# Storing the last sample of a four-layer convolution kernel in sixteen blocks instead of one transfer

## The chip, the cores and the metric

The kernel runs on one core of a Trainium2 chip. The metric is the device time of one execution in microseconds (us), lower being better. The engines are named as in the profile: PE (TensorE, matrix multiplication), DVE (VectorE), ACT (ScalarE), POOL (GpSimd) and SP (SyncE, which here only issues transfers). Each has its own instruction stream, and they meet at semaphores. SP and ACT can both issue DMAs, each on a queue of its own; the profile calls these instructions SPq and ACTq DMA_DIRECT2D.

## The reference

The input is x, eight samples of 16 channels of 128x128 float32. Four residual layers follow one another, each on a group-normalised copy of x:

```python
x = x + _L0_conv_ref(_gn(x), ...)   # 3x3 conv, kernel mixed per sample from 3 experts
x = x + _L1_conv_ref(_gn(x), ...)   # abs, then 3x3 depthwise conv
x = x + _L2_conv_ref(_gn(x), 8)     # 17x17 box mean
x = x + _L3_conv_ref(_gn(x), ...)   # neighbour sums, then five 1x1 convs, elu between them
```

In the last layer the sums of the eight neighbours go through four 64-wide layers with elu, and a fifth that is averaged and scaled down to 16 channels. Only its result, added to x, completes an output sample. The output has the shape of x, 1 MB per sample.

## The kernel before, in words

All eight samples stay in one SBUF tile `xs` of 128 partitions. A partition holds one channel c and one residue r of the image row modulo 8 (`R = 8`, `C = 16`), and in it lie `K = 16` rows of 128 values for each sample. The layout of a sample in DRAM, seen the same way, is `ov` (L209): r, c, k, w, in which one run of adjacent bytes is one image row of 512 bytes. A sample is worked on in `Q = 4` quarters of `KB = 4` such rows per partition.

The work is a software pipeline over samples, written out by hand for every engine in a function `one(t)` that `rounds` calls (L288): round t finishes sample t-1's last layer while the earlier layers of samples t, t+1 and t+2 run beside it. In the last round (t = 8) only the last layer of sample 7 is left. That layer goes, for each quarter and each of its layers, from PE (`layer`, L764) to ACT and DVE (`elu`, L646, and `join`, L979), and back to PE. The fifth layer is `last_layer` (L785), and `output` (L989) on DVE adds its result into `xs` and increments `out_evac`. Quarters 0, 1 and 2 of the last sample are written by DVE inside the last round; the fourth comes after it, as the last instruction of the DVE stream.

SP issues the transfers in this order: within a round the load of a later sample, the store of an earlier one, then the windows and stacks that spread neighbouring rows over partitions. `store(j)` (L387) waits until all four quarters of sample j are in `xs` and then issues one DMA of the whole sample:

```python
def store(j):
    sp.wait_ge(out_evac, Q * j + Q)
    sp.dma_start(ov[j] if isinstance(j, int) else ..., xs[:, bass.ds(j * N, N)]...).then_inc(out_stored, 16)
```

Sample 6 is stored in the last round, and `store(B - 1)` for sample 7 stands behind `rounds` (L430). The last wait of SP (L431) is for all eight stores. ACT's stream ends with its part of the last round; it issued DMAs only during the start of the kernel.

Of the kernel before, what the change touches and what calls it, by code (L numbers as in the profile page):

```python
# [16 lines left out]
B, C, H, W = 8, 16, 128, 128  # L17
R = 8
K = H // R
P = R * C  # L20
N = K * W
Q = 4
KB = K // Q
# [52 lines left out]
def build(nc, x, w_experts, conv_bias, fc_w, fc_b, w_depth, w1, w2, w3, w4, w5, con_early, con_channel, con_late, out):  # L76
    with ExitStack() as ctx:
        def sb(name, shape, dtype=F32):
            return ctx.enter_context(nc.sbuf_tensor(name, shape, dtype))
# [4 lines left out]
        def sem(name):  # L84
            return ctx.enter_context(nc.semaphore(name))
# [6 lines left out]
        xs = sb("xs", [P, B * N])  # L92
# [112 lines left out]
        out_evac = sem("out_evac")  # L205
        out_stored = sem("out_stored")

        xv = x.rearrange("b c (k r) w -> b r c k w", r=R)
        ov = out.rearrange("b c (k r) w -> b r c k w", r=R)  # L209
# [26 lines left out]
        LOAD = 16  # L236
# [37 lines left out]
        def loaded(i):  # L274

            return LOAD if isinstance(i, int) and i == 0 else LOAD * (i + 2)

        def has(i):

            return not isinstance(i, int) or 0 <= i < B  # L280
# [7 lines left out]
        def rounds(eng, one):  # L288

            one(1)  # L290
            with eng.Fori(2, B - 3) as t:
                one(t)
            for t in range(B - 3, B + 1):
                one(t)
# [32 lines left out]
        def windows0(eng, i, halves, last):  # L327

            for h in halves:
                eng.wait_ge(y0_written, Y0 * i + Y0 // 2 * (h + 1))  # L330
                for dst, rows in around(y0, win0, h, False):
                    eng.dma_start(dst, rows).then_inc(win0_in, 16)
                dst, rows = ((win0[1][3 * C:4 * C, K - 1:K], y0[6 * C:7 * C, K - 1:K]) if h else
                             (win0[0][0:C, 0:1], y0[C:2 * C, 0:1]))
                eng.dma_start(dst, rows).then_inc(win0_in, 16)
            if last:
                eng.wait_ge(y0_written, Y0 * i + Y0)
                for h in range(2):
                    for dst, rows in around(y0, win0, h, True):
                        eng.dma_start(dst, rows).then_inc(win0_in, 16)  # L340

        def windows1(eng, i, halves, last):

            for h in halves:
                eng.wait_ge(y1_written, Y1 * i + 2 * h + 2)
                for dst, rows in around(y1, win1, h, False):
                    eng.dma_start(dst, rows).then_inc(win1_in, 16)
            if last:
                eng.wait_ge(y1_written, Y1 * i + Y1)
                for h in range(2):  # L350
                    for dst, rows in around(y1, win1, h, True):
                        eng.dma_start(dst, rows).then_inc(win1_in, 16)

        def stacks(eng, i, h):

            eng.wait_ge(near_rows, Q * i + 2 * h + 2)
            if not (isinstance(i, int) and i == 0):
                eng.nop(nofuse=True)
                eng.wait_ge(z_mm, zn(i - 1, 2 * h + 1, 0, M - 1))
                eng.nop(nofuse=True)  # L360
            lo, hi = h * K // 2, (h + 1) * K // 2
            up, down = max(lo, 1), max(lo - 1, 0)
            for m in range(M):
                a, b = max(2 * m - 1, 0), min(2 * m + 3, R)
                top, bottom = C * (a - 2 * m + 1), C * (b - 2 * m)
                eng.dma_start(stack[m][top:3 * C, lo:hi], near_sum[C * a:C * (2 * m + 2), lo:hi]).then_inc(stack_in[h], 16)
                eng.dma_start(stack[m][3 * C:5 * C, lo:hi], y3[2 * C * m:2 * C * m + 2 * C, lo:hi, 1:W + 1]).then_inc(stack_in[h], 16)
                eng.dma_start(stack[m][5 * C:5 * C + bottom, lo:hi], near_sum[2 * C * m:C * b, lo:hi]).then_inc(stack_in[h], 16)
            eng.dma_start(stack[0][0:C, up:hi], near_sum[7 * C:P, up - 1:hi - 1]).then_inc(stack_in[h], 16)
            eng.dma_start(stack[3][7 * C:P, down:hi - 1], near_sum[0:C, down + 1:hi]).then_inc(stack_in[h], 16)  # L370

        block = ctx.enter_context(nc.Block())


        @block.sync
        def _(sp):
            def load(i):
                src = xv[i] if isinstance(i, int) else xv[bass.ds(i, 1)].rearrange("b r c k w -> (b r) c k w")
                sp.dma_start(xs[:, bass.ds(i * N, N)].rearrange("p (k w) -> p k w", w=W), src).then_inc(x_loaded, 16)

            def load_rows(i, first, end):
                sp.dma_start(xs[first * C:end * C, i * N:(i + 1) * N].rearrange("p (k w) -> p k w", w=W),
                             xv[i][first:end]).then_inc(x_loaded, 16)

            load(0)
            sp.dma_start(tables[0], con_early).then_inc(s_early, 16)
            def store(j):  # L387
                sp.wait_ge(out_evac, Q * j + Q)
                sp.dma_start(ov[j] if isinstance(j, int) else ov[bass.ds(j, 1)].rearrange("b r c k w -> (b r) c k w"),
                             xs[:, bass.ds(j * N, N)].rearrange("p (k w) -> p k w", w=W)).then_inc(out_stored, 16)  # L390

            def one(t):
                if has(t + 3):
                    sp.wait_ge(x_loaded, loaded(t + 2))
                    sp.nop(nofuse=True)
                    load(t + 3)
                if has(t - 2):
                    store(t - 2)
                if has(t + 1):
                    sp.wait_ge(conv_mm[1], 2 * (t + 1))  # L400
                    sp.nop(nofuse=True)
                    windows1(sp, t + 1, range(2), True)
                if has(t + 2):
                    sp.wait_ge(conv_mm[0], 2 * (t + 2))
                    sp.nop(nofuse=True)
                    windows0(sp, t + 2, range(2), True)
                if has(t):
                    stacks(sp, t, 0)
                    stacks(sp, t, 1)

            sp.wait_ge(x_loaded, LOAD)
            sp.dma_start(tables[2], con_late).then_inc(s_late, 16)
            load_rows(1, 0, R // 2)
            sp.wait_ge(zeroed, N_ZEROED)
            windows0(sp, 0, (0,), True)
            load_rows(1, R // 2, R)
            sp.wait_ge(x_loaded, LOAD * 3)
            load(2)
            windows1(sp, 0, (0,), True)
            sp.wait_ge(conv_mm[0], 2)  # L420
            windows0(sp, 1, (0,), True)
            sp.wait_ge(x_loaded, loaded(2))
            load(3)
            sp.wait_ge(conv_mm[0], 4)
            windows0(sp, 2, range(2), True)
            sp.wait_ge(conv_mm[1], 2)
            windows1(sp, 1, (0,), True)
            stacks(sp, 0, 0)
            rounds(sp, one)
            store(B - 1)  # L430
            sp.wait_ge(out_stored, B * LOAD)  # L431


        @block.gpsimd
# [168 lines left out]
        def _(act):  # L603
# [85 lines left out]
            windows1(act, 1, (1,), False)  # L689
            stacks(act, 0, 1)  # L690
            rounds(act, one)


        @block.tensor
# [517 lines left out]
```

## Time and profile before

| | us |
|---|---|
| three executions | 733.02, 736.15, 737.25 |
| their median | 736.15 |
| the profiled execution | 733.21 |
| its span, first to last instruction | 731.4 |

| engine | busy us | share of the span |
|---|---|---|
| PE | 603.0 | 82% |
| DVE | 580.0 | 79% |
| ACT | 554.8 | 76% |
| POOL | 316.2 | 43% |

The span is what the trace covers; 1.8 us of the profiled execution lie outside it. Times in rows are counted from the span's start. The DMA share is the mean busy share of the core's 16 DMA engines. DMA-issuing instructions aren't counted in an engine's busy time. In the column PEclk the page gives the TensorE clock that was granted, as a share of full speed.

### The profile page before, as it was taken

The numbers are of one execution on the slowest core, as the hardware profiler recorded it, in microseconds if no ns is written. First come the engines' busy times: TensorE is split into PE (matmuls) and PEld (weight loads), VectorE is DVE, ScalarE is ACT, GpSimd is POOL, SyncE is SP. The second block draws the span as 40 slices with busy tenths as digits, with TensorE's granted clock in tenths as the row PEclk, the third lists the DMA queues.
The fourth block names the chain that finished last, engine by engine and source line by source line (L and its number), as shares of the span: only waits on it lengthen the run. The fifth ranks groups of instructions, "written<-read, shape, count | busy, mean of one in ns | idle before, by whom it ended". The sixth has DMA issues, their size and how long they took to land.

```text
span 731.4 us, 13381 instructions
## 1 busy us (share of the span) xinstructions
PE 603.0 (82%) x4142; PEld 166.1 (23%) x4142; DVE 580.0 (79%) x1006; ACT 554.8 (76%) x1057; POOL 316.2 (43%) x487
## 2 busy tenths in 40 slices
PE   0351863599999999999999999999999899889982
PEld 0210221122222222222222222222222222222220
DVE  1342576398998989898989898988888788799992
ACT  0212210289999999999999999999999999988881
POOL 2304015616791579157915791579006800720000
PEclk9995796899999999999999999999999999999996
DMA  5739769807385928693859285719530830182002
GB/s 104 137 74 171 137 147 200 162 12 159 77 200 116 210 54 188 130 199 59 201 126 207 42 192 128 162 40 199 131 75 8 201 81 0 36 198 55 1 1 57
DMA packets 72867, 85.53 MB, mean 117 GB/s; under 512 B 8675, under 2 KB 58355, under 8 KB 72819
## 3 DMA queue, kind: packets, MB, share of 16 engines
q1 hardware_dynamic: 68096, 78.58, 50.2%
q10 hardware_dynamic: 4722, 6.34, 4.8%
q8 instruction: 26, 0.43, 0.3%
q14 instruction: 23, 0.18, 0.1%
HBM read 9.14 MB, written 8.39 MB: 24 GB/s over the span
## 4 chain that ended last, share of the span: by engine, by line
PE 44%; DVE 27%; ACT 12%; issue 8%; DMA 5%; ACTq 1%; DVEq 1%; POOL 1%; POOLq 0%
PE pz L782 20%; PE pc L728 9%; DVE g L986 8%; PE pc L759 7%; ACT u L651 5%; DVE bn L929 4%; ACT u L654 4%; DVE u L983 3%; DVE g_last L986 3%; ACT u L657 3%; DMA win<-y 3%; PE po L728 3%; PE po L791 2%; DVE box_sum L1002 2%; DVE xs L970 2%
## 5 line engine op out<-in xcount | busy, mean ns | idle before, releaser
L651 ACT ACTIVATE u<-pz 128x512 f32<-128x512 f32 x472 | 260.5, 601 | 61.4 <-PE pz L782 59.0
L782 PE MATMUL pz<-g,wT 64*64 64x512 f32 x1536 | 272.3, 610 | 18.6 <-DVE g L986 16.7
L986 DVE SCALAR_TENSOR_TENSOR g<-u,pz 128x512 f32<-128x512 f32 x384 | 247.8, 680 | 39.4 <-ACT u L654 34.9
L654 ACT ACTIVATE u<-u 128x512 f32<-128x512 f32 x472 | 275.7, 640 | 1.3
L759 PE MATMUL pc<-win,t 64*32 64x512 f32 x1392 | 100.2, 652 | 28.4 <-DMA win<-y 12.7
L782 PEld LDWEIGHTS pz<-g,wT 64*64 64x64 f32 x1536 | 69.1, 131 | 197.5 <-issue 195.9
L929 DVE BATCH_NORM_STATS2 bn<-xs 128x6 f32<-128x512 f32 (+1 forms) x128 | 84.4, 684 | 19.9 <-DMA xs<-in_x_dram 17.3
L986 DVE SCALAR_TENSOR_TENSOR g_last<-u,pz 128x512 f32<-128x512 f32 x128 | 82.7, 681 | 21.0 <-ACT u L654 19.3
L782 PE MATMUL pz<-stack,wT 64*64 64x512 f32 x512 | 86.7, 619 | 10.7 <-issue 4.9
L728 PE MATMUL pc<-box_sum,box_mat 128*128 128x512 f32 x138 | 74.6, 635 | 1.2 <-DVE box_sum L1002 0.8
L453 POOL TENSOR_TENSOR stat<-stat 128x1 f32<-128x1 f32 x32 | 6.2, 193 | 154.8 <-DVE stat L944 154.8
L638 ACT ACTIVATE y<-xs,stat 128x512 f32<-128x512 f32 (+1 forms) x32 | 25.7, 820 | 45.1 <-POOL stat L463 45.1
L700 PE MATMUL psm<-stat,con 128*128 128x2 f32 x64 | 12.7, 269 | 42.3 <-DVE stat L937 42.2
L511 POOL TENSOR_TENSOR y<-xs,stat 128x512 f32<-128x512 f32 x20 | 20.8, 1040 | 60.1 <-DVE box_sum L1002 60.1
L1002 DVE TENSOR_TENSOR_SCAN box_sum<-y 128x580 f32<-128x580 f32 x32 | 43.2, 1359 | 0.0
L759 PEld LDWEIGHTS pc<-win,t 64*32 64x32 f32 x1392 | 19.9, 112 | 98.8 <-issue 98.8
L791 PE MATMUL po<-g_last,w5T 128*32 128x512 f32 x256 | 35.0, 619 | 2.9 <-DVE g_last L986 2.9
L550 POOL TENSOR_TENSOR near_sum<-near_sum,box_sum 128x512 f32<-128x512 f32 x30 | 35.5, 1182 | 4.3 <-DVE near_sum L1030 2.0
L782 PEld LDWEIGHTS pz<-stack,wT 64*64 64x64 f32 x512 | 19.8, 132 | 64.8 <-issue 64.5
L728 PEld LDWEIGHTS pc<-box_sum,box_mat 128*128 128x128 f32 x138 | 21.5, 188 | 53.0 <-issue 44.1
L657 ACT ACTIVATE u<-u 128x512 f32<-128x512 f32 x40 | 25.2, 630 | 10.7 <-DVE u L983 10.4
L546 POOL TENSOR_TENSOR near_sum<-box_sum 128x512 f32<-128x512 f32 x30 | 31.7, 1058 | 1.8 <-DVE box_sum L1009 1.8
(96 smaller groups left out, 486.9 us busy)
## 6 DMA issues: line engine op xcount, KB each, us to landing
stack<-near_sum SPq DMA_DIRECT2D x90, 192.0 KB, 3.9
win<-y SPq DMA_DIRECT2D x56, 260.0 KB, 4.5
win<-y SPq DMA_DIRECT2D x56, 195.0 KB, 4.5
out_dram<-xs SPq DMA_DIRECT2D x8, 1024.0 KB
stack<-box_sum SPq DMA_DIRECT2D x60, 128.0 KB, 3.8
xs<-in_x_dram SPq DMA_DIRECT2D x7, 1024.0 KB
stack<-near_sum SPq DMA_DIRECT2D x30, 128.0 KB, 2.7
win<-y ACTq DMA_DIRECT2D x8, 260.0 KB, 8.0
```

The lines of the kernel that those rows point to most:

```text
L546: pool.tensor_tensor(o, y[:, :, 0:W], y[:, :, 1:W + 1], ALU.add).then_inc(near_pairs_done, 1)
L550: pool.tensor_tensor(o, o, y[:, :, 2:W + 2], ALU.add).then_inc(near_rows, 1)
L651: act.activation(u[:, m, :], pz[:, m, :], ACT.Relu, scale=-1.0, bias=0.0).then_inc(relu_done, 1)
L654: act.activation(u[:, m, :], u[:, m, :], ACT.Exp, scale=-1.0).then_inc(exp_done, 1)
L657: act.activation(u[:, 2 * a + 1, :], u[:, 2 * a + 1, :], ACT.Exp).then_inc(exp_done, 1)
L728: mm = pe.matmul(chunk_bank(i, c), box_mat[:, d, :], box_sum[:, c * KB + d:(c + 1) * KB + d, RAD:RAD + W], start=d == 0, stop=d == 2)
L759: last = pe.matmul(pair_banks(i, k, n)[2 * C * m:2 * C * m + 2 * C, h, :], mat[rows, kw, :], blocks(win[m // 2], n + 2 * h)[rows, :, kw:kw ...
L782: last = pe.matmul(pz[to, m, :], wT[rows, l, rows], src, start=True, stop=True)
L791: last = pe.matmul(po[32 * m:32 * m + 32, :], w5T[:, :], elus(LAYERS - 1)[:, m, :], start=True, stop=True)
L929: dve.bn_stats(bn[k][:, c, :], sample(i, c)).then_inc(stat_step[k], 1)
L986: dve.scalar_tensor_tensor(out=elus(l)[:, m, :], in0=u[:, m, :], scalar=-1.0, in1=pz[:, m, :], op0=ALU.add, op1=ALU.max).then_inc(g_writte ...
L1002: dve.tensor_tensor_scan(own_rows(box_sum, c).rearrange("p k w -> p (k w)"), y2[:, c * n + BOX:(c + 1) * n + BOX], y2[:, c * n:(c + 1) * n ...
```

## The change

Sample 7 is no longer stored by one DMA. A new helper `store_blocks(eng, j, first, end)` waits until the quarter that holds row block end-1 is written, and then issues one DMA per k, each of one row of 512 bytes from each of the 128 partitions (64 KB). SP calls it for the blocks of quarters 0, 1 and 2, four blocks each, and then for the first two blocks of the fourth quarter. ACT, behind its last round, issues the other two. SP's last wait is for seven whole stores and sixteen blocks. The stores of samples 0 to 6 are as before.

```diff
+        def store_blocks(eng, j, first, end):
+
+            eng.wait_ge(out_evac, Q * j + (end - 1) // KB + 1)
+            for k in range(first, end):
+                eng.dma_start(ov[j][:, :, k, :], xs[:, j * N + k * W:j * N + (k + 1) * W]).then_inc(out_stored, 16)
...
@@ block.sync
             rounds(sp, one)
-            store(B - 1)
-            sp.wait_ge(out_stored, B * LOAD)
+            for q in range(Q - 1):
+                store_blocks(sp, B - 1, q * KB, (q + 1) * KB)
+            store_blocks(sp, B - 1, K - KB, K - KB // 2)
+            sp.wait_ge(out_stored, (B - 1 + K) * LOAD)
...
@@ block.scalar
             rounds(act, one)
+            store_blocks(act, B - 1, K - KB // 2, K)
```

## Rows read from the trace of the kernel before

**Rows 1.** The page: span, then DMA share in 40 slices and GB/s.
```profile
span 731.4 us, 13381 instructions
DMA  5739769807385928693859285719530830182002
GB/s 104 137 74 171 137 147 200 162 12 159 77 200 116 210 54 188 130 199 59 201 126 207 42 192 128 162 40 199 131 75 8 201 81 0 36 198 55 1 1 57
```

**Rows 2.** The chain that ended last, its end: start us, us, what.
```profile
716.96 0.70 DVE g_last L986
717.66 0.14 issue
717.80 1.97 PE po L791 x8
719.77 0.02 issue
719.79 0.69 DVE xs L991
```

**Rows 3.** Waits of SP's queue from 657 us on.
```profile
SPq L389 <- DVE xs L991: 63.3, 1, 63.3
SPq L77 <- DMA out_dram<-xs: 9.8, 1, 9.8
```

**Rows 4.** Timeline of SP, the last two stores: start us, us, what.
```profile
656.47 0.71 SPq L389 DMA_DIRECT2D out_dram<-xs  x1
...
720.51 0.69 SPq L389 DMA_DIRECT2D out_dram<-xs  x1
```

**Rows 5.** Windows, the end: PE, PEld, DVE, ACT, POOL busy, PEclk, DMA share, GB/s.
```profile
720.50:721.20 0.70, 0.00 (x0) 0.00 (x0) 0.00 (x0) 0.00 (x0) 0.00 (x0) 0.50 0.00 0
721.20:722.20 1.00, 0.00 (x0) 0.00 (x0) 0.00 (x0) 0.00 (x0) 0.00 (x0) 0.50 0.17 39
722.20:723.20 1.00, 0.00 (x0) 0.00 (x0) 0.00 (x0) 0.00 (x0) 0.00 (x0) 0.50 0.47 100
...
728.20:729.20 1.00, 0.00 (x0) 0.00 (x0) 0.00 (x0) 0.00 (x0) 0.00 (x0) 0.50 0.56 164
729.20:730.20 1.00, 0.00 (x0) 0.00 (x0) 0.00 (x0) 0.00 (x0) 0.00 (x0) 0.50 0.39 114
730.20:731.40 1.20, 0.00 (x0) 0.00 (x0) 0.00 (x0) 0.00 (x0) 0.00 (x0) 0.50 0.04 11
```

**Rows 6.** Timeline of SP, issues in a row while ACT issues none.
```profile
645.11 0.59 SPq L370 DMA_DIRECT2D stack<-near_sum  x1
645.84 0.51 SPq L366 DMA_DIRECT2D stack<-near_sum  x1
646.39 0.63 SPq L367 DMA_DIRECT2D stack<-box_sum  x1
```

**Rows 7.** Timeline of ACT, issues while SP issues too.
```profile
119.05 0.53 ACTq L366 DMA_DIRECT2D stack<-near_sum  x1
119.60 0.81 ACTq L367 DMA_DIRECT2D stack<-box_sum  x1
120.44 1.32 ACTq L368 DMA_DIRECT2D stack<-near_sum  x1
```

**Rows 8.** DMA issues: KB each, median us from issue to landing.
```profile
win<-y SPq DMA_DIRECT2D x56, 195.0 KB, 4.5
stack<-near_sum SPq DMA_DIRECT2D x14, 64.0 KB, 2.9
```

**Rows 9.** Windows of 10 us of the last round, columns as in Rows 5.
```profile
656.50:666.50 10.00, 8.81 (x41) 2.16 (x40) 9.49 (x16) 8.56 (x15) 0.00 (x0) 1.00 0.49 121
666.50:676.50 10.00, 8.87 (x48) 2.00 (x47) 9.58 (x16) 8.35 (x15) 0.00 (x0) 1.00 0.00 1
```

**Rows 10.** Timeline of DVE, L983 with a store running (first two), without (last two).
```profile
660.20 0.68 DVE L983 TENSOR_SCALAR u<-pz 128x512 f32<-128x512 f32 x1
662.18 0.68 DVE L983 TENSOR_SCALAR u<-pz 128x512 f32<-128x512 f32 x1
...
684.61 0.68 DVE L983 TENSOR_SCALAR u<-pz 128x512 f32<-128x512 f32 x1
686.60 0.68 DVE L983 TENSOR_SCALAR u<-pz 128x512 f32<-128x512 f32 x1
```

**Rows 11.** Timeline of DVE, the first three quarters' outputs.
```profile
674.09 0.68 DVE L991 TENSOR_TENSOR xs<-po,xs 128x512 f32<-128x512 f32 x1
...
694.54 0.68 DVE L991 TENSOR_TENSOR xs<-po,xs 128x512 f32<-128x512 f32 x1
...
707.04 0.68 DVE L991 TENSOR_TENSOR xs<-po,xs 128x512 f32<-128x512 f32 x1
```

**Rows 12.** Timeline of ACT, its last instruction.
```profile
716.30 0.63 ACT L657 ACTIVATE u<-u 128x512 f32<-128x512 f32 x1 [0.21 <-DVE u L983]
```

## The prediction

> **What bounds the kernel now.** Only the stretch that the change touches matters, so I read the views from the end backwards. The page first: the DMA engines are almost idle from about 603 us on, but for the last stacks with the store of sample 6 behind them, and the very last slice [rows 1]. The end of the chain of waits comes next: DVE's g_last, the eight matmuls of the fifth layer, and DVE's addition into xs, which ends at 719.79 + 0.69 = 720.48 [rows 2]. No engine computes after that. The waits of SP tell what the rest is: it sat 63.3 us at the store of sample 7, until DVE's last addition, then issued it at 720.51, and then waited 9.8 us for its data [rows 3, 4]. So from 720.51 to the span's end at 731.4, 10.9 us, the kernel does nothing but store one megabyte, three quarters of which had been ready before: quarters 0, 1 and 2 were written at 674.8, 695.2 and 707.7 [rows 11].
>
> The windows of the tail cut these 10.9 us into three. The first packets: the window from 721.2 moved 39 KB, at the 100 GB/s of the next one 0.39 us of work, so data began at about 722.2 - 0.39 = 721.8, that is **1.3 us** after the issue began. The data: the window from 730.2 moves only 1.2 x 11 = 13 KB, 0.1 us at the 114 GB/s before it, so the data ended at about 730.3; **8.5 us** for 1.05 MB, 123 GB/s in the mean, from 100 at the beginning to 164 near the end. The rest, 731.4 - 730.3 = **1.1 us**, is landing, SP's wake-up and the end (the issue ended at 721.2 and the wait took 9.8, so SP was released at 731.0: 0.7 us for the landing, 0.4 for the end) [rows 1, 3 to 5].
>
> **The change part by part.**
>
> *Twelve blocks of quarters 0 to 2, on SP.* They leave the tail with 786 KB. Where they go: SP has nothing else to do in those 63 us [rows 3], and the DMA engines have nothing between the end of sample 6's store and 720 (share 0.00, 1 GB/s) [rows 9]. Each quarter costs SP four issues. An issue in a row takes 0.51 to 0.63 us and 0.04 between them [rows 6], so 4 x 0.65 = 2.6 us. Its 262 KB at 100 GB/s take 2.6 us beside that, starting 1.3 us after the first issue; a quarter is out some 5 to 6 us after it was written. The gaps between quarters are 20.5, 12.5 and 12.8 us [rows 2, 11], so every burst is over before the next, and the third, begun at 707.7, by about 713.5, 7 us ahead of the last block. Cost on the path: 0. The cover is that idle time; if it were missing, the third burst would delay the last quarter by up to its 2.6 us.
>
> *Do the bursts slow the chain of DVE and ACT that runs meanwhile?* The store of sample 6 answers it, since it ran in the same loop at 121 GB/s: the starts of L983 are 662.18 - 660.20 = 1.98 us apart with it, and 686.60 - 684.61 = 1.99 without [rows 9, 10]. So 0, and for the upper bound 0.01 us in each of the some 23 periods from 674.8 on, 0.2 us.
>
> *Four blocks of the last quarter, two on SP and two on ACT.* ACT ended its last activation at 716.93 [rows 12], is idle, and waits for the same increment as SP, and nothing is queued behind its DMAs. Both start issuing at about 720.5. The second issue begins 0.55 us later, and its own packets 1.3 us after that, at 722.4; where both queues issue, the second instruction on ACT took 0.81 us instead of 0.63 and the third 1.32 [rows 7], so perhaps 0.2 us later. By then the first two blocks have begun (721.8) and, with 131 KB at 100 GB/s, they last until 723.1, so no gap opens. The data of the four: 262 KB at 100 GB/s, 2.6 us, to 724.4. I take 100, since a transfer has the slow rate at its beginning [rows 5] and this one is over in the time of that beginning. Then the same 1.1 us: the span ends at 725.5.
>
> The bounds of this term. The fastest rate of the tail, 164 GB/s, gives 1.6 us of data, but the second blocks can't be out before 722.4 + 131 KB / 164 = 723.2, and the end is 724.3. On the slow side stands what one block can cost by itself: 64 KB stacks take 2.9 us from issue to landing and window transfers 4.5 us, among heavy traffic [rows 8]; a block issued at 721.1 to 721.3 that took 4.5 would land at 725.8 and end the span at 726.2.
>
> *The trade of one DMA for four in the tail, seen by the skill.* The trace has, for one DMA, 1.3 us before its data and 0.7 behind [rows 3 to 5], paid once if the four overlap. The Trainium skill (DMA: Bandwidth & Descriptors, section "Rules for kernel authors") speaks against the change: transfers under 64 KB pay mostly overhead and full bandwidth wants 1 MiB in one; the same page gives a fixed cost of about 2.0 us per DMA, which agrees with the trace's 1.3 + 0.7. What that rule would do here, if the fixed cost were paid block after block, is rivals C and D.
>
> *Sum.* Removed: 8.5 us of data in the tail; added: 2.6; the fixed parts stay: 2.6 - 8.5 = **-5.9 us**, bounds -7.1 and -5.2. The span goes from 731.4 to 725.5 and the profiled execution from 733.21 to 727.3. That execution was a low one of its kernel: the median shown is 736.15, 2.9 us higher, and since the tail is a fixed piece of either, I subtract the same 5.9: **730.2 us**.
>
> **The rivals.**
>
> *A. All sixteen DMA engines take part.* In the tail the share never passes 0.56 while data flows without a break [rows 5]: eight of sixteen at work. Were a block of 128 rows spread over sixteen, the four would need 1.3 us of data, bound by the second issue: 722.4 + 0.7 + 1.1 = 724.2, so -7.2 us, 729.0. For it: the pattern of a block is a dimension shorter. Against it: its outermost dimension in DRAM is still r, with eight entries. The Trainium skill (DMA: Bandwidth & Descriptors, section "Why a DMA increments its semaphore by 16 and not by 1") says that the number of engines is the largest up to 16 that divides the outermost dimension of both sides, here eight before and after; by it, A doesn't happen, and the trace agrees for before.
>
> *B. Blocks of one queue follow one another.* If the second block of a queue began only when the first had landed, each pair would take 1.3 + 1.3 + 0.7 = 3.3 us, twice that and 0.4 for the end is 7.0 instead of 10.9: -3.9 us, 732.2. Against it: stacks are issued every 0.65 us and each takes 2.9 and more to land, so several are in flight on one queue [rows 6, 8].
>
> *C. All four follow one another,* over both queues, at 2.9 us each [rows 8]: 4 x 2.9 + 0.4 = 12.0 instead of 10.9, +1.1 us, 737.3: no change that can be told.
>
> *D. Slower: the same mechanism at a higher price.* Its place is the same four blocks; at the 4.5 us of a window transfer [rows 8] they take 18.4 us, +7.5, 743.6. It ends above the time before from (10.9 - 0.4) / 4 = 2.6 us per block on. Against C and D stand the same rows as against B, and the two queues.
>
> *E. The bursts slow the chain.* Three bursts of some 5.5 us lie beside it. Were everything under them a third slower, 5.5 us would be lost, and -5.9 becomes -0.4: 735.8. Rows 10 speak against it, with 1.98 against 1.99 us.
>
> **How the numbers follow.** Chances: the forecast 0.77, A 0.06, B 0.09, C 0.03, D 0.02, E 0.03. The range: the forecast's bounds on the slowest and the quickest of the three executions give 733.0 - 7.1 = 725.9 and 737.25 - 5.2 = 732.0; A lies inside, and B's 732.2 is taken in with a little for its spread: 726.0 to 732.8. A measurement of this kernel can tell about 0.5% (3.7 us) from no change. The forecast and A are past it by 2 us or more, of which I take 0.02 off for the spread of the executions (4.2 us before), and half of B is: 0.77 + 0.06 - 0.02 + 0.05 = 0.86 faster. Within: the other half of B, C, E and those 0.02: 0.12. Slower: D, 0.02.
>
> **What would show it.** In the windows of the new end, data at half share from about 1.3 us after the last addition, for 2 to 3 us, and then nothing; SP's last wait down from 9.8 us to 3 to 4. Three separate bursts of 262 KB near 675, 696 and 709 us, and L983 still 1.98 us apart in them. The last addition should still start near 719.8: if it's later, E is at work. A share near 1.0 in the tail would show A, and two or four humps with gaps B, C or D. The step most likely to be off is the rate of the last 262 KB, since rows of a block lie further apart in DRAM than those of a whole sample and two queues share the engines.

## The result and the profile after

| | before, us | after, us |
|---|---|---|
| median, six executions each | 737.58 | 729.38 |
| lowest to highest | 733.02 to 738.92 | 728.08 to 731.78 |
| profiled execution's span | 731.4 | 726.3 |

The ratio of after to before is 0.9901, with a 95% interval of 0.9873 to 0.9929: 0.7 to 1.3% faster. On 737.58 us the ratio is -7.3 us, with -5.2 to -9.4 as its interval. The two medians lie further apart, 8.2 us. The time forecast was 730.2, the difference forecast -5.9.

The spans of the two profiled executions differ by 5.1 us, which is two things of opposite sign. First the end of the chain of waits after, in the same columns as [rows 2] (start us, us, what):

```profile
719.69 0.70 DVE g_last L995
720.39 0.14 issue
720.52 1.10 PE po L800 x8
721.62 0.02 issue
721.64 0.69 DVE xs L1000
```

The last addition ends at 722.33, 1.85 us *later* than the 720.48 of before. From there to the end of the span it is 726.28 - 722.33 = 3.95 us, where before had 10.9. The **tail**, counted like this, is the measure used below: it shrank by 7.0 us. SP's waits after, as in [rows 3] (waited for: us in total, times, longest):

```profile
SPq L376 <- DVE xs L1000: 53.8, 4, 17.8
SPq L77 <- DMA out_dram<-xs: 2.2, 1, 2.2
```

The one wait of 63.3 us has become four, and the last wait for data fell from 9.8 to 2.2 us. (53.8 and 63.3 aren't the same stretch: before's ran from the end of the last issue, after's has the early issues taken out.) The stores' instructions after, first the timeline of SP at the first burst, then of SP and of ACT at the end (start us, us, what):

```profile
677.50 2.69 SPq L376 DMA_DIRECT2D out_dram<-xs  x4
```

```profile
722.36 1.30 SPq L376 DMA_DIRECT2D out_dram<-xs  x2
```

```profile
722.37 1.52 ACTq L376 DMA_DIRECT2D out_dram<-xs  x2
```

And the windows of the tail after, with the columns of [rows 5] (the five engines' busy time, PEclk, DMA share, GB/s):

```profile
722.20:723.20 1.00, 0.00 (x0) 0.00 (x0) 0.14 (x1) 0.00 (x0) 0.00 (x0) 0.72 0.00 0
723.20:724.20 1.00, 0.00 (x0) 0.00 (x0) 0.00 (x0) 0.00 (x0) 0.00 (x0) 0.50 0.30 78
724.20:725.20 1.00, 0.00 (x0) 0.00 (x0) 0.00 (x0) 0.00 (x0) 0.00 (x0) 0.50 0.55 157
725.20:726.30 1.10, 0.00 (x0) 0.00 (x0) 0.00 (x0) 0.00 (x0) 0.00 (x0) 0.50 0.09 25
```

Read them as the prediction read before's: 78 KB at 157 GB/s are 0.50 us, so data began at 723.7, 1.3 us after the first issue (722.36), as before. The last window's 1.1 x 25 = 27.5 KB are 0.2 us of it, so by the amount moved the data ended at about 725.4 to 725.5: 1.8 us of data for 262 KB, then 0.8 us to the end.

Finer windows of both ends show where the last packets were, first before, then after:

```profile
730.20:730.70 0.50, 0.00 (x0) 0.00 (x0) 0.00 (x0) 0.00 (x0) 0.00 (x0) 0.50 0.09 27
730.70:731.40 0.70, 0.00 (x0) 0.00 (x0) 0.00 (x0) 0.00 (x0) 0.00 (x0) 0.50 0.00 0
```

```profile
725.40:725.60 0.20, 0.00 (x0) 0.00 (x0) 0.00 (x0) 0.00 (x0) 0.00 (x0) 0.50 0.09 26
725.60:726.28 0.68, 0.00 (x0) 0.00 (x0) 0.00 (x0) 0.00 (x0) 0.00 (x0) 0.50 0.00 0
```

The single DMA still moved packets until about 730.7, a few at a time; the blocks ended by 725.6. From the last packet to the end of the span both kernels take about the same, 0.7 us. Counted up to the last packet, the data took 8.8 us before (721.8 to 730.7) and 1.9 us after (723.6 to about 725.5).

The first burst (quarter 0) shows in the windows after, and the L992 of DVE beside it (that was L983 of before, [rows 10]):

```profile
678.50:679.50 1.00, 0.69 (x4) 0.22 (x4) 0.90 (x3) 0.97 (x3) 0.00 (x0) 1.00 0.25 67
679.50:680.50 1.00, 1.00 (x6) 0.22 (x4) 1.00 (x2) 0.79 (x2) 0.00 (x0) 1.00 0.47 127
680.50:681.50 1.00, 0.88 (x6) 0.22 (x4) 0.90 (x3) 0.97 (x3) 0.00 (x0) 1.00 0.31 85
681.50:683.00 1.50, 1.38 (x8) 0.45 (x8) 1.40 (x3) 1.29 (x3) 0.00 (x0) 1.00 0.00 0
```

```profile
679.37 0.68 DVE L992 TENSOR_SCALAR u<-pz 128x512 f32<-128x512 f32 x1
...
681.35 0.68 DVE L992 TENSOR_SCALAR u<-pz 128x512 f32<-128x512 f32 x1
...
683.34 0.68 DVE L992 TENSOR_SCALAR u<-pz 128x512 f32<-128x512 f32 x1
```

The starts are 1.98 and 1.99 us apart, under the burst and behind it.

**Where the 1.85 us come from.** Not from the last round. The output additions after are at these starts:

```profile
676.79 0.68 DVE L1000 TENSOR_TENSOR xs<-po,xs 128x512 f32<-128x512 f32 x1
697.25 0.68 DVE L1000 TENSOR_TENSOR xs<-po,xs 128x512 f32<-128x512 f32 x1
709.76 0.68 DVE L1000 TENSOR_TENSOR xs<-po,xs 128x512 f32<-128x512 f32 x1
```

Against [rows 11] the first is 2.70 us late, and the gaps of 20.46 and 12.51 us are before's 20.45 and 12.50. The lateness is older: an addition of the start-up, where the two programs are the same, has it already (DVE's timeline, before and then after):

```profile
124.36 1.29 DVE L973 TENSOR_TENSOR xs<-pc,xs 128x512 f32<-128x512 f32 x2 [4.54 <-PE pc L759]
```

```profile
126.70 1.29 DVE L982 TENSOR_TENSOR xs<-pc,xs 128x512 f32<-128x512 f32 x2 [4.97 <-PE pc L768]
```

It is 2.34 us late there. The last layer's eight matmuls gave 0.87 us back: 1.10 us at a granted clock of 1.00 (2.4 GHz) in the windows from 720.5 to 721.7, against 1.97 us [rows 2] at 0.50 (1.2 GHz) in the window from 717.8 to 719.8. In both, PE had been idle for 2.9 us before them. That isn't the change's doing: in the profiles of the eight kernels below, all of which store in another form than before, these matmuls took 1.97 us seven times and 1.85 once.

In all ten profiles the last addition ended between 718.7 and 726.2 us, in no order with what the kernel did to the stores. Nearly all of this spread is older than 146.3 us: the granted clock rose to 1.00 for the long stretch of the rounds at 138.6 to 146.3 us (140.1 before, 142.4 after), and the last addition ended 579.3 to 580.4 us after that in every one of the ten. So the tails are compared from traces, and the times carry the spread of the start-up.

### The profile page after: what moved, and what is told of

The parts are those of the page before. It is cut to its first block, busy times and chain, and to the rows that moved or that the text cites. A ratio compares the mean times of both kernels' runs of the same rounds, so it can differ in the third digit from the quotient of the medians.

```text
span 726.3 us, 13396 instructions
## 1 busy us (share of the span) xinstructions
PE 602.0 (83%) x4142; PEld 166.2 (23%) x4142; DVE 580.2 (80%) x1006; ACT 555.4 (76%) x1057; POOL 316.9 (44%) x487
## 4 chain that ended last, share of the span: by engine, by line
PE 43%; DVE 27%; ACT 12%; issue 9%; DMA 5%; ACTq 1%; DVEq 1%; POOL 1%; POOLq 0%
PE pz L791 20%; PE pc L737 9%; DVE g L995 8%; PE pc L768 7%; ACT u L659 5%; DVE bn L938 4%; ACT u L662 4%; DVE u L992 3%; DVE g_last L995 3%; DMA win<-y 3%; ACT u L665 3%; PE po L737 3%; DVE box_sum L1011 2%; PE po L800 2%; DVE xs L979 2%
## 5 line engine op out<-in xcount | busy, mean ns | idle before, releaser
L709 PE MATMUL psm<-stat,con 128*128 128x2 f32 x64 | 12.7, 269 | 44.2 <-DVE stat L946 44.1
```

## The experiments

Each diff is against the changed kernel; `...` stands for lines left out. The first kernel took the split apart by queue.

**All blocks on SP.**

```diff
-            for q in range(Q - 1):
+            for q in range(Q):
                 store_blocks(sp, B - 1, q * KB, (q + 1) * KB)
-            store_blocks(sp, B - 1, K - KB, K - KB // 2)
...
-            store_blocks(act, B - 1, K - KB // 2, K)
```

> All sixteen blocks on SP's queue, four per quarter as each is written; ACT stores nothing. Theory (blocks of one queue overlap, the end is set by the issues and by one queue's data rate): last issue begins 4 x 0.65 - 0.65 = 1.95 us after the first, its packets 1.25 us later, the data end about 3.8 us after DVE's last addition, and the tail from that addition to the span's end is 4.5 to 4.8 us, against 4.0 in the changed kernel: 0.5 to 0.8 us worse than it, still some 6 us under the 10.9 of before. Rival (a queue's blocks follow one another, landing before the next begins): 4 x (1.3 + 0.3 + 0.4) + 0.4, a tail of 8.4 us.

Ratio to before 0.9903 (0.9877 to 0.9928), median 729.43. The trace (last addition, then SP's timeline, then windows):

```profile
724.37 0.69 DVE L998 TENSOR_TENSOR xs<-po,xs 128x512 f32<-128x512 f32 x1 [2.14 <-PE po L798]
725.09 2.63 SPq L376 DMA_DIRECT2D out_dram<-xs  x4
```

```profile
726.30:726.90 0.60, 0.00 (x0) 0.00 (x0) 0.00 (x0) 0.00 (x0) 0.00 (x0) 0.50 0.41 109
726.90:727.50 0.60, 0.00 (x0) 0.00 (x0) 0.00 (x0) 0.00 (x0) 0.00 (x0) 0.50 0.39 108
727.50:728.10 0.60, 0.00 (x0) 0.00 (x0) 0.00 (x0) 0.00 (x0) 0.00 (x0) 0.50 0.36 96
728.10:728.70 0.60, 0.00 (x0) 0.00 (x0) 0.00 (x0) 0.00 (x0) 0.00 (x0) 0.50 0.34 88
```

The tail is 729.67 - 725.06 = 4.6 us, as the first theory had it. Data flows without a gap while blocks are issued 2.63 / 4 = 0.66 us apart, so a queue's blocks overlap and rival B falls. The share of 0.34 to 0.41 is below the half that saturates eight engines: one queue that begins a block every 0.66 us (65.5 KB, 99 GB/s) doesn't feed them. ACT's share in the change is worth 0.66 us of the 7.0 by the two traces; the times (729.43 and 729.38) can't tell it.

**All sixteen blocks late, on two queues.**

```diff
-            for q in range(Q - 1):
-                store_blocks(sp, B - 1, q * KB, (q + 1) * KB)
-            store_blocks(sp, B - 1, K - KB, K - KB // 2)
+            sp.wait_ge(out_evac, Q * B)
+            store_blocks(sp, B - 1, 0, K // 2)
...
-            store_blocks(act, B - 1, K - KB // 2, K)
+            act.wait_ge(out_evac, Q * B)
+            store_blocks(act, B - 1, K // 2, K)
```

> All sixteen blocks wait for the last quarter, and then go out eight on SP and eight on ACT: the same DMAs, none early. It parts the gain into being early and being cut and on two queues. Theory A (two queues move data faster than one: 157 GB/s in the changed kernel's tail): 1.05 MB / 157 = 6.7 us, with 1.3 before and 0.8 behind a tail of 8.8 us, unless the issues set it: eight at 0.65 to 0.9 are 5.2 to 7.2 us, and the end 7 to 9. Theory B (the rate is that of the rows of before, 123 GB/s, and the 157 came of a short transfer): 8.5 + 2.1 = 10.6 us, as before.

Ratio 0.9979 (0.9962 to 0.9996). Its last addition, issues and four windows of its data:

```profile
725.48 0.69 DVE L1000 TENSOR_TENSOR xs<-po,xs 128x512 f32<-128x512 f32 x1 [2.14 <-PE po L800]
726.20 5.64 SPq L376 DMA_DIRECT2D out_dram<-xs  x8
726.25 5.95 ACTq L376 DMA_DIRECT2D out_dram<-xs  x8
```

```profile
727.50:728.50 1.00, 0.00 (x0) 0.00 (x0) 0.00 (x0) 0.00 (x0) 0.00 (x0) 0.50 0.53 145
728.50:729.50 1.00, 0.00 (x0) 0.00 (x0) 0.00 (x0) 0.00 (x0) 0.00 (x0) 0.50 0.55 159
729.50:730.50 1.00, 0.00 (x0) 0.00 (x0) 0.00 (x0) 0.00 (x0) 0.00 (x0) 0.50 0.57 166
...
732.50:733.50 1.00, 0.00 (x0) 0.00 (x0) 0.00 (x0) 0.00 (x0) 0.00 (x0) 0.50 0.56 157
```

The tail is 735.17 - 726.17 = 9.0 us, theory A. The same megabyte in blocks from two queues runs at 145 to 166 GB/s from its first full window on, where the single DMA ran at 100 there [rows 5], with eight engines nearly saturated in both (0.53 and 0.47). So 1.9 us of the tail come of cutting and of the second queue together (on one queue the cut alone costs time, as the kernel with all sixteen blocks on SP shows below), and the 5.1 from 9.0 to 3.95 of twelve blocks being early.

**The whole sample late, by residue.**

```diff
+        def store_residues(eng, j, first, end, need):
+
+            eng.wait_ge(out_evac, need)
+            for r in range(first, end):
+                eng.dma_start(ov[j][r], xs[r * C:(r + 1) * C, j * N:(j + 1) * N].rearrange("p (k w) -> p k w", w=W)).then_inc(out_stored, 16)
...
+            store_residues(sp, B - 1, 0, R // 2, Q * B)
...
+            store_residues(act, B - 1, R // 2, R, Q * B)
```

> The whole last sample waits for the last quarter and goes out as eight DMAs of 128 KB, one per residue r (16 partitions, outermost dimension 16 on both sides), four on SP and four on ACT. Theory (a DMA whose outermost dimension is 8 runs on eight of the sixteen engines, and that bounds the tail of before): the DMA share goes over 0.56 towards 1, the rate to 250 GB/s or more, data about 4.2 us, tail 6 to 6.5 us. Rival (the write to DRAM or something shared bounds it): share up, rate at about 160 GB/s, tail 8.7 us.

Ratio 0.9958 (0.9938 to 0.9979). Its issues and three windows of its data:

```profile
723.26 3.51 SPq L382 DMA_DIRECT2D out_dram<-xs  x4
723.27 4.66 ACTq L382 DMA_DIRECT2D out_dram<-xs  x4
```

```profile
725.60:726.60 1.00, 0.00 (x0) 0.00 (x0) 0.00 (x0) 0.00 (x0) 0.00 (x0) 0.50 0.92 184
726.60:727.60 1.00, 0.00 (x0) 0.00 (x0) 0.00 (x0) 0.00 (x0) 0.00 (x0) 0.50 0.96 258
727.60:728.60 1.00, 0.00 (x0) 0.00 (x0) 0.00 (x0) 0.00 (x0) 0.00 (x0) 0.50 1.01 256
```

The share reaches 1.01 and the rate 258 GB/s, so the store before was bound by its eight engines, and the write to DRAM bears more than 166 GB/s. That is what [rows 5] had suggested with their 0.56 at most, and what the Trainium skill's rule (DMA: Bandwidth & Descriptors, section "Why a DMA increments its semaphore by 16 and not by 1") says: the engines of a DMA number the largest divisor up to 16 of both outermost dimensions. The sizes agree with it here, 8 and then 16. The tail was 730.91 - 723.23 = 7.7 us, though, more than the 6 to 6.5 expected: the first microsecond of data moved only 93 GB/s at a share of 0.73, the next 184. The issues weren't even either: SP's four took 0.9 us each in the mean and ACT's 1.2, where blocks took 0.7. Which of the two held the data back wasn't tried.

**The early blocks left out.** Quarters 0 to 2 of the last sample aren't stored.

```diff
-            for q in range(Q - 1):
-                store_blocks(sp, B - 1, q * KB, (q + 1) * KB)
```

> The twelve blocks of quarters 0 to 2 of the last sample are left out (that part of the output isn't written); the last four go out as in the changed kernel. Theory (the early blocks are hidden wholly): tail 4.0 us as in the changed kernel, L-groups of DVE's last layer still 1.98 us apart, and the time the same as the changed kernel's within 0.3%. Rival (the early bursts slow the chain or shift it by the 1.85 us by which the changed kernel's last addition came later than before's): the last addition comes about 1.9 us earlier, and the kernel is about 2 us faster than the changed one.

Ratio 0.9899 (0.9875 to 0.9924), median 729.42 against the changed kernel's 729.38, with a tail of 4.0 us. Its output additions:

```profile
678.11 0.68 DVE L998 TENSOR_TENSOR xs<-po,xs 128x512 f32<-128x512 f32 x1
698.56 0.68 DVE L998 TENSOR_TENSOR xs<-po,xs 128x512 f32<-128x512 f32 x1
711.07 0.68 DVE L998 TENSOR_TENSOR xs<-po,xs 128x512 f32<-128x512 f32 x1
```

The gaps are 20.45 and 12.51 us, those of a kernel that stores beside them, and the last addition came later still (724.50) than in the changed kernel. The twelve early blocks cost nothing that the gaps or the times can show, and the rival that they shift the chain falls.

**The last addition in two halves.** `store_block` waits for the number of quarters or halves that it is given, and issues one block.

```diff
-            output(B - 1, Q - 1)
+            dve.wait_ge(out_mm, Q * B)
+            for h in range(2):
+                at = (B * K - KB + 2 * h) * W
+                dve.tensor_tensor(xs[:, at:at + 2 * W], po[:, 2 * h * W:2 * (h + 1) * W], xs[:, at:at + 2 * W], ALU.add).then_inc(out_evac, 1)
...
+            store_block(sp, K - 4, Q * B)
+            store_block(sp, K - 2, Q * B + 1)
...
+            store_block(act, K - 3, Q * B)
+            store_block(act, K - 1, Q * B + 1)
```

> As the changed kernel, but DVE writes the last quarter in two halves of 256 columns, and each half's two blocks go out as soon as it is written, one on SP and one on ACT. Theory (the tail is a fixed 2.0 us, the issues and the data of four blocks): counted from DVE's start of the last addition the changed kernel needs 4.7 us; here the first pair is issued about 0.3 us earlier and the second right behind it on each queue, so 4.3 to 4.4 us; 0.3 us can't be seen in the times, but in the trace. Rival (two short additions and two waits cost as much as they bring): 4.7 us or more.

Ratio 0.9896 (0.9865 to 0.9927), median 729.20. Its end:

```profile
724.84 0.76 DVE L1205 TENSOR_TENSOR xs<-po,xs 128x256 f32<-128x256 f32 x2 [2.02 <-PE po L808]
725.29 1.30 SPq L382 DMA_DIRECT2D out_dram<-xs  x2
725.30 1.53 ACTq L382 DMA_DIRECT2D out_dram<-xs  x2
```

From the start of the addition to the end of the span it is 729.24 - 724.84 = 4.4 us; the changed kernel has 726.28 - 721.64 = 4.64. So 0.24 us were gained, as expected. This is the quickest form of those tried by the trace, and by the times it can't be told from the changed kernel.

**The last quarter by residue, in eight DMAs.**

```diff
+            for r in range(first, end):
+                eng.dma_start(ov[j][r, :, K - KB:K, :], xs[r * C:(r + 1) * C, (j + 1) * N - CH:(j + 1) * N].rearrange("p (k w) -> p k w", w=W)).then_inc(out_stored, 16)
...
+            last_quarter(sp, B - 1, 0, R // 2)
...
+            last_quarter(act, B - 1, R // 2, R)
```

> Quarters 0 to 2 as in the changed kernel; the last quarter goes out as eight DMAs of 32 KB, one per residue (outermost dimension 16), four on each queue. Theory (for 262 KB the issues set the end, not the number of DMA engines): the fourth issue of a queue begins about 2.2 us after the first, and the tail is 4.5 to 5 us, worse than the 4.0 of four blocks, though the DMA share may pass 0.56. Rival (engines set it): data in about 1 us, tail 3.2 us.

Ratio 0.9915 (0.9883 to 0.9948). Issues and windows:

```profile
723.18 1.77 SPq L382 DMA_DIRECT2D out_dram<-xs  x4
723.19 1.84 ACTq L382 DMA_DIRECT2D out_dram<-xs  x4
```

```profile
724.00:725.00 1.00, 0.00 (x0) 0.00 (x0) 0.00 (x0) 0.00 (x0) 0.00 (x0) 0.50 0.58 132
725.00:726.00 1.00, 0.00 (x0) 0.00 (x0) 0.00 (x0) 0.00 (x0) 0.00 (x0) 0.50 0.55 130
```

The tail is 3.8 us, so my 4.5 to 5 were wrong, and the rival's 3.2 too. I had priced the issue at 0.65 us whatever the DMA; these take 1.77 / 4 = 0.44. That the issues set the pace holds: two queues give 2 x 32.8 KB per 0.44 to 0.46 us, some 145 GB/s, and the windows show 132 at a share of 0.58, well short of what sixteen engines moved above. The tail is even 0.2 us under the changed kernel's 3.95, since the data began sooner, 0.8 us after the first issue instead of 1.3; the times can't tell the two apart.

**All sixteen blocks late, on SP alone.**

```diff
+            sp.wait_ge(out_evac, Q * B)
+            store_blocks(sp, B - 1, 0, K)
...
-            store_blocks(act, B - 1, K - KB // 2, K)
```

> All sixteen blocks wait for the last quarter and go out on SP's queue alone. Theory (an issue costs 0.66 us and bounds one queue at about 65.5 KB per 0.66 us = 99 GB/s): last issue 15 x 0.66 = 9.9 us after the first, then 1.3 + 0.4 + 0.7: a tail of 12.3 us, 1.4 us longer than the one DMA of before. Rival (the blocks' shorter packets on eight engines keep 150 GB/s whatever the queue): 9 us, as with two queues. Rival (landing before the next begins): over 25 us.

Ratio 1.0046 (1.0018 to 1.0074): slower than before. Its end:

```profile
718.02 0.69 DVE L998 TENSOR_TENSOR xs<-po,xs 128x512 f32<-128x512 f32 x1 [2.14 <-PE po L798]
718.80 10.71 SPq L376 DMA_DIRECT2D out_dram<-xs  x16
```

The issues alone last 10.71 us, 0.67 each, and the tail 731.41 - 718.71 = 12.7 us, 1.8 more than the one DMA needed. Cutting has a price: 0.67 us per block on its queue. The change escapes most of it, since twelve of the sixteen are issued where SP is idle and the rest by two queues.

**The last quarter left out.** Its four blocks aren't stored; SP still waits for the last addition.

```diff
-            store_blocks(sp, B - 1, K - KB, K - KB // 2)
+            sp.wait_ge(out_evac, Q * B)
...
-            store_blocks(act, B - 1, K - KB // 2, K)
```

> The four blocks of the last quarter are left out (that part of the output isn't written); SP still waits for the last addition. It shows what is left to gain in the tail. Theory: tail 0.4 to 0.6 us, so the time is 3.4 us under the changed kernel's, some 10.5 us under that of before.

Ratio 0.9871 (0.9837 to 0.9905), median 725.42; the tail is 720.42 - 720.00 = 0.4 us, which bounds what any further work on this store could bring at 3.5 us. By the medians it is 4.0 us under the changed kernel, where 3.4 had been expected.

## Why the prediction was right

| step | predicted, us | measured, us |
|---|---|---|
| early blocks, on the path | 0 | 0 (1.98 us periods; 729.42 without them) |
| first issue to first data | 1.3 | 1.3 |
| data of the last 262 KB | 2.6 | 1.9 to its last packet (1.8 by amount) |
| data of the one DMA, taken away | 8.5 | 8.8 to its last packet |
| landing and end | 1.1 | 0.7, before as after (last packet to end) |
| tail | 10.9 to 5.0 | 10.9 to 3.95 |
| difference | -5.9 | -7.0 by the trace, -7.3 by the ratio, -8.2 between the medians |

- **What bounds the end** was right: a store in which no engine computes, three quarters of it ready long before. Putting all blocks late took away 5.1 of the 7.0 us.
- **The cover of the early blocks** was right. SP's four issues took 2.69 us against 2.6 worked out, and the burst was over 4 us after it began. Rival E falls by the untouched gaps, and by the kernel without those blocks. The sign that was set for it, a last addition later than 719.8, did appear (721.64); it came of the start-up, and would have misled whoever went by it alone.
- **The rate of the last 262 KB was the mis-sized term.** I took 100 GB/s, "since a transfer has the slow rate at its beginning". That isn't so of every transfer: sixteen blocks from two queues start at 145 GB/s. It cost 0.7 to 0.8 us. I named this step as the likeliest to be off, but looked for the slower side. Whether the quicker packets come of the order of rows in a block or of the second queue isn't settled: SP alone moved 88 to 109 GB/s at a share of 0.34 to 0.41, about 265 GB/s for a full share, against 213 in the first full window of the single DMA (100 / 0.47) and 285 with two queues (157 / 0.55). That speaks for the form of the blocks as the larger part, but only against the beginning of the single DMA: near its end that moved 293 by the same reckoning (164 / 0.56). Sample 6's single DMA did the same, 97 GB/s at a share of 0.45 from 658.5 to 659.5 us and 171 at 0.57 from 664.5 to 665.5. Why that form begins slowly is open.
- **The other 0.3 us are data too.** The prediction let the single DMA's data end at 730.3 and put the rest into landing and end. Its packets went on until 730.7, so 8.8 us were taken away and not 8.5; landing and end are 0.7 us in both kernels. The prediction's "0.7 for the landing" is therefore some 0.3 from the last packet to SP's release at 731.0, and one DMA's fixed part up to its landing is 1.3 + 0.3 = 1.6 us here. The Trainium skill's fixed cost of about 2.0 us (DMA: Bandwidth & Descriptors, section "Anatomy of one DMA — SWDGE (gpsimd) path") is a fit for transfers issued from GpSimd; the prediction called it in agreement with a DMA issued by SP, and these rows put it somewhat lower.
- **The lower bound of the tail** worked with 164 GB/s gave -7.1, and the trace's -7.0 is next to it, in part by luck: it had the data end 2.7 us after the first issue and the span 1.1 us behind that, and measured were 3.2 and 0.7.
- **Signs.** Data flowed for 1.9 us where 2 to 3 were named, and SP's last wait was 2.2 us where 3 to 4 were named.
- **Rival A** (sixteen engines): no, the share stayed at 0.55. **B, C, D** (one block after another): no, the data has no gaps, even on one queue. D's turning point in another guise did come true where it was built on purpose: late and on one queue the blocks are slower than the single DMA, by their issues and not by their landings. The Trainium skill (DMA: Bandwidth & Descriptors, section "Rules for kernel authors") advises to coalesce many small transfers into one large one, and names 64 KB, which is just the size of a block; that late run agrees (12.7 us against 10.9), and the change, with its issues hidden or shared, does not (3.95).
- **The time** of 730.2 is 0.8 us above the 729.38 measured. That is closer than it deserves. Before's median rose by 1.4 us, from 736.15 to 737.58, with three more executions; the difference was 1.1 us (trace) to 1.4 us (ratio) larger than forecast, which cancels that; and the medians lie 0.9 us further apart than the ratio gives, well within the spread of the executions.

## What to carry to other kernels

When a kernel ends in a wait for a store, measure the time from the last computing instruction to the end, and send out early whatever part of the output is ready; only the last piece, a fixed part of some 2 us and its own data, needs to stay. Cut only where the issues are hidden or split over queues, since each cost 0.4 to 0.8 us on its queue here, and up to 1.2 in the mean in the residue form. Look at the DMA share while only one transfer runs: 0.5 at full flow meant here that half of the engines took no part, and another outermost dimension brought them in, to a share of 1.01. For the last 262 KB that brought no shorter data, since the issues set its pace.

## What the runs showed of the hardware

- The same megabyte, from SBUF to DRAM in runs of 512 bytes: some 120 GB/s in the mean as one DMA over eight engines, 145 to 166 as sixteen blocks from two queues on as many, up to 258 as eight DMAs over sixteen engines. That the same eight engines move more when the transfer is cut and shared by two queues I hadn't expected.
- The issue of a DMA isn't one price: 0.66 us for 128 runs of 512 bytes on SP, 0.44 for 64 runs. It isn't proportional to the runs either: the whole sample, 2048 runs, took 0.69 [rows 4], and the eight residue DMAs of 256 runs 0.9 (SP) and 1.2 us (ACT) in the mean. With the shorter issue the data also began sooner: in the last kernel by residue its first full window starts 0.8 us after the issue began, against 1.3 in the changed kernel and before.
- The last addition ended anywhere in 718.7 to 726.2 us in ten profiled executions, but 579.3 to 580.4 us after the granted clock's last rise to 1.00 in each. In the pair compared here the difference was there by 124 us; why the start-up varies so was not tried.
